# GpSimd scales and sums the gathered rows of a token tile; VectorE adds one finished sum

## The chip, the cores and the metric

The kernel runs on one core of a Trainium2 chip. The metric is device time in microseconds: the median over runs of the whole program. A TensorE, a VectorE, a ScalarE, a GpSimd and a SyncE engine work side by side in the core, each in the order of its own queue, and wait for each other on semaphores.

## What is computed

Two layers over 4 sequences of 512 tokens, width 512: a state-space mixer, a mixture of experts (64 experts, 8 for each token), a cross-attention with 16 heads, and a feed-forward part with quantized weights. The change lies in the attention stage, which also carries the end of the expert part: each token's 8 expert rows are fetched from memory, weighted and added to the residual x. In the reference, cut to that:

```python
y = lax.ragged_dot(hact, jnp.swapaxes(down_proj, 1, 2), group_sizes)
w = top_val.reshape(-1)[order]
out = jnp.zeros_like(x).at[tok].add(y * w[:, None])     # 8 rows per token
...
x = x + _L0_ffn_ref(_layernorm(x, axis=-1), ...)
x = x + _L1_xattn_ref(_layernorm(x, axis=-1), ctx_1024, ...)
...
q = rmsnorm((hidden_states @ Wq).reshape(B, Sq, H, D), gq)
scores = jnp.einsum('bqhd,bkhd->bhqk', q, k) * scale
attn = jax.nn.softmax(scores, axis=-1)
out = jnp.einsum('bhqk,bkhd->bqhd', attn, v).reshape(B, Sq, H * D) @ Wo
```

## The kernel before

`attention` (from L1421) works through 64 **units**: batch b = unit // 16, head = unit % 16. Every engine has a function `unit(pp, k)` that says, in the order of the code, what it does in a unit; nothing reorders it, so the order of the code is the order of each queue. In one unit:

- **TensorE** makes the scores of 4 query tiles (into `ps_s`, two banks), the value product of the unit before (`ps_o`), the q product of the next unit (`ps_q`), the transposes of the probabilities (`turn`, L1601), a part of the output product (`output`) and the sums of squares for the next q (`q_sums`, L1582).
- **VectorE** takes the row maxima (L1885) and makes `neg` from them and `q_rs` (L1893), takes reciprocals of the softmax sums (L1901), makes the low halves of q, prob and o (`low`, L1869), adds an output part into X (L1917) and makes `q_ms` (L1875).
- **ScalarE** takes the exponential (L1713) and the high halves (L1687).
- **GpSimd** makes the low halves of k and v (`k_part` L1779, `v_part` L1785), divides the probabilities (`normalize`, L1797) and takes the root `q_rs` (`q_root`, L1791). The root belongs to the next unit and is the last thing that the next maxima's `neg` needs.

Into this the tokens of the *next* batch are woven, for batches 0 to 2. They come as 32 rows (4 tiles of 128 tokens, 8 rows each), three per unit, in units 0 to 10 of a batch (`arriving(u, i)` names row number g, tile t and place kk among the 8). For each, GpSimd issues an indirect DMA (`gather`, L1805) from `y_dram` into one of RING = 4 slots of `got_row`, and VectorE scales it and accumulates it into X in one instruction (`gather_add`, L1928): one row ahead of the second pair of maxima, one between the first and the second `prob_t_low`, one between the third and the fourth. The three `gather` of a unit stand ahead of the first pair of `normalize`, after `v_part`, and behind `q_root`; each waits for the slot's last reader (semaphore `added`). When a tile is complete, its layer norm follows one step per unit, by `token_tile(u, lag)` and the table `STATS = (2, 5, 8, 10)`:

- lag 0, end of unit 2, 5, 8 or 10: `token_stats` on VectorE (L1937 and on),
- lag 1, the unit after: `token_root` on GpSimd (L1813), `token_norm` on VectorE (`nbias` L1971, `xn` L1975),
- lag 2: `turn_token` on TensorE, copies on ScalarE and VectorE into `x_t`.

In batches 1 to 3 the finished tiles of the batch before get their statistics in units 4 to 7 (`ended_stats`, L1953) and a root on GpSimd in unit 9. The q product of the next batch's first unit needs all four tiles.

GpSimd waits through `pool_waits`, an instruction of its own that stands in its queue. The accumulation of before:

```python
dve.wait_ge(arrived[g % RING], 16 * (g // RING + 1))
wait(dve, added, g)
dve.scalar_tensor_tensor(out=c.X[:, t, :], in0=got[:, g % RING, :],
                         scalar=m.weight[:, t, kk:kk + 1], in1=c.X[:, t, :],
                         op0=ALU.mult, op1=ALU.add).then_inc(added, 1)
```

## Time and profile before

| | us |
|---|---|
| median of 3 runs (3116.88 to 3126.09) | 3119.8 |
| the profiled execution | 3117.0 |
| its span, first to last instruction | 3115.6 |
| TensorE busy (80%) | 2485.5 |
| VectorE busy (65%) | 2025.2 |
| GpSimd busy (51%) | 1586.5 |
| ScalarE busy (40%) | 1250.8 |

The attention stage runs from about 1912 to 2920 us of the span. A share of busy time is a mean over stages with different limits; for the stage in question the rows further down show single stretches and single units. "Idle before" a group is time in which its engine waited just ahead of its instructions, with the instruction that ended the wait.

### The profile page before, as it was taken

What the parts mean: (1) busy time and instruction counts of PE and PEld (TensorE: products, weight loads), DVE (VectorE), ACT (ScalarE), POOL (GpSimd) and SP (SyncE); (2) the same over time, 40 slices, a digit from 0 to 9 for tenths busy, and PEclk for the clock granted to TensorE, in tenths of its full rate; (3) what the DMA queues carried; (4) which work ended last, traced back from release to release, by engine and by line L of the source; (5) the groups of instructions that cost most, each with busy time, mean ns of one, the idle gap of its engine ahead of it and who ended that gap; (6) DMA issues with size and microseconds to landing.
All of it is one profiled execution on the core that took longest, in us unless ns stands there. A gap on an engine that the chain in (4) does not pass through costs nothing. (4 is left out here: it accounts for less than half of the span.)

```text
span 3115.6 us, 42764 instructions
## 1 busy us (share of the span) xinstructions
PE 2485.5 (80%) x11156; PEld 1737.0 (56%) x11174; DVE 2025.2 (65%) x3184; ACT 1250.8 (40%) x2245; POOL 1586.5 (51%) x1294
## 2 busy tenths in 40 slices
PE   7825655555979489999999983889989999999686
PEld 2301212214767367667777762677777777877443
DVE  3579999897868334554444446675776676565596
ACT  3424343443345232221121212545545545555365
POOL 2446565564047666666666626654664655444110
PEclk9869899898989799999999996999999999999899
DMA  2016666653369798887777745443443543342101
GB/s 84 9 41 214 219 210 223 219 202 118 141 238 339 264 316 287 306 277 247 247 235 255 248 148 180 145 139 126 146 140 105 166 139 115 95 136 82 54 0 54
DMA packets 260696, 538.30 MB, mean 173 GB/s; under 512 B 24401, under 2 KB 90065, under 8 KB 259809
## 3 DMA queue, kind: packets, MB, share of 16 engines
q1 hardware_dynamic: 207296, 347.98, 32.9%
q0 software_dynamic: 44032, 167.80, 16.3%
q10 hardware_dynamic: 9248, 21.11, 2.0%
q8 instruction: 54, 0.88, 0.1%
q14 instruction: 66, 0.53, 0.1%
HBM read 328.14 MB, written 208.67 MB: 172 GB/s over the span
## 5 line engine op out<-in xcount | busy, mean ns | idle before, releaser
L523 PE MATMUL ps_y<-c_state,ident 128*128 128x512 f32 x512 | 268.7, 651 | 205.5 <-DVE c_state L475 205.4
L448 POOL TENSOR_TENSOR b_u<-du,bc 128x1024 f32<-128x1024 f32 x128 | 301.3, 2354 | 214.5 <-DVE c_state L475 178.0
L1713 ACT ACTIVATE prob<-ps_s,neg,q_rs 128x512 f32<-128x512 f32 x256 | 197.1, 774 | 330.5 <-DVE neg L1893 330.5
L1230 PE MATMUL ps_o<-w_dn,hid_t 96*128 x632 | 308.4, 611 | 0.0
L1797 POOL TENSOR_SCALAR prob<-prob,rden 128x512 f32<-128x512 f32 x256 | 175.6, 696 | 253.9 <-DVE rden L1901 253.9
L523 PEld LDWEIGHTS ps_y<-c_state,ident 128*128 128x128 f32 x512 | 91.8, 198 | 381.8 <-DVE c_state L475 312.7
L467 DVE TENSOR_TENSOR_SCAN state<-ps_decay,b_u 128x1024 f32<-128x1024 f32 x128 | 293.1, 2290 | 16.1 <-issue 8.7
L1266 ACT ACTIVATE silu_g<-ps_gu 128x192 f32<-128x192 f32 x159 | 52.6, 331 | 546.5 <-PE ps_gu L1211 543.0
L419 ACT ACTIVATE ps_decay<-delta,a_neg 128x511 f32 x256 | 165.9, 681 | 225.5 <-DVE state L467 225.1
L1211 PE MATMUL ps_gu<-w_gu_high,rows_t_high 128*128 (+1 forms) x636 | 230.7, 363 | 11.0 <-POOL w_gu_low L1095 9.5
L1095 POOL TENSOR_TENSOR w_gu_low<-raw_gu,w_gu_high 128x1536 fp32r<-128x1536 f32 x64 | 222.4, 3475 | 12.0 <-POOL w_gu_high L1093 12.0
L1352 DVE TENSOR_TENSOR hid<-silu_g,ps_gu 128x192 f32<-128x192 f32 x159 | 56.2, 354 | 250.4 <-ACT silu_g L1266 250.4
L1211 PE MATMUL ps_gu<-w_gu_high,rows_t_low 128*128 (+1 forms) x636 | 216.0, 340 | 0.0
L1211 PE MATMUL ps_gu<-w_gu_low,rows_t_high 128*128 (+1 forms) x636 | 215.8, 339 | 0.0
L913 POOL DMA_INDIRECT rows_dram<-xn,pos_row x128 | 126.8, 991 | 149.8 <-issue 149.8
L1687 ACT ACTIVATE prob_t_high<-ps_p 128x512 fp32r<-128x512 f32 x256 | 143.4, 607 | 130.3 <-PE ps_p L1601 130.0
L1346 DVE TENSOR_TENSOR rows_t_low<-ps_rx,rows_t_high 128x512 fp32r<-128x512 f32 x160 | 110.7, 692 | 128.1 <-ACT rows_t_high L1260 128.1
L1869 DVE TENSOR_TENSOR prob_t_low<-ps_p,prob_t_high 128x512 fp32r<-128x512 f32 x256 | 169.6, 682 | 32.7 <-ACT prob_t_high L1687 32.2
L1558 PE MATMUL ps_q<-x_t,w_q 128*128 128x512 f32 x768 | 189.6, 396 | 1.5 <-DVE x_t L1869 1.5
L475 DVE TENSOR_TENSOR c_state<-state,bc 128x1024 f32<-128x1024 f32 x128 | 189.9, 1485 | 0.0
L1558 PEld LDWEIGHTS ps_q<-x_t,w_q 128*128 128x128 f32 x768 | 147.2, 192 | 33.7 <-issue 1.9
L1885 DVE TENSOR_REDUCE high<-ps_s 128x1 f32<-128x512 f32 x256 | 163.5, 678 | 1.1 <-PE ps_s L1558 0.9
(317 smaller groups left out, 6071.5 us busy)
## 6 DMA issues: line engine op xcount, KB each, us to landing
rows_dram<-zeros SPq DMA_DIRECT2D x15, 3584.0 KB, 14.3
raw_gu<-in_gate_up POOLq DMA_DIRECT2D x64, 768.0 KB, 5.4
rows<-rows_dram SPq DMA_DIRECT2D x160, 256.0 KB, 3.9
y_dram<-y SPq DMA_DIRECT2D x158, 256.0 KB, 3.5
bc<-bc_dram SPq DMA_DIRECT2D x64, 512.0 KB, 5.8
w_q<-wq_dram SPq DMA_DIRECT2D x64, 512.0 KB, 3.7
w_o<-wo_dram SPq DMA_DIRECT2D x16, 2048.0 KB, 8.5
w_dn<-in_down POOLq DMA_DIRECT2D x64, 384.0 KB, 5.9
```

What stands on the lines that cost most here:

```text
L419: e = act.activation(decay[ec % 2][:, g * SEQ + 1:(g + 1) * SEQ], m.delta[:, ds1(b * EC + ec), 1:].rearrange("p a l -> p (a l)"), ACT.Exp, ...
L448: pool.tensor_tensor(out=b_u[:, ec % 2, :, :], in0=m.du[:, ds1(b * EC + ec), :].broadcast_to([P, G, SEQ]), in1=bc[:, par, 0, :, :], op=ALU ...
L467: dve.tensor_tensor_scan(state[:, ec % 2, :], decay[ec % 2][:, :], b_u[:, ec % 2, :, :].rearrange("p g l -> p (g l)"), 0.0, ALU.mult, ALU. ...
L475: dve.tensor_tensor(out=c_state[:, ec % 2, :, :], in0=state[:, ec % 2, :].rearrange("p (g l) -> p g l", g=G), in1=bc[:, par, 1, :, :], op= ...
L523: mm = pe.matmul(ps_y[ec][:, :], c.ident[:, :], c_state[:, ec % 2, g, :], start=False, stop=False)
L1095: pool.tensor_tensor(out=flat(w_gu[1]), in0=raw_gu[slot][:, :], in1=flat(w_gu[0]), op=ALU.subtract).then_inc(gu_ready, 1)
L1211: mm = pe.matmul(ps_gu[par][:, :], rows_t[par][x][:, k, :], w_gu[w][:, ds1(slot), k, :].rearrange("p a f -> p (a f)"), start=n == 0, stop= ...
L1230: mm = pe.matmul(ps_o[par][:, :], hid_t[par][:, k, :], w_dn[:, ds1(slot), k, :].rearrange("p a f -> p (a f)"), start=k == 0, stop=k == 1)
L1558: mm = pe.matmul(out, lhs[a], rhs[b], start=i == 0, stop=i == n - 1)
L1713: act.activation(prob[:, qt, :], ps_s[qt % 2][:, :], ACT.Exp, scale=q_rs[:, k % 2, qt:qt + 1], bias=neg[:, qt:qt + 1], accum_out=den[:, qt ...
L1797: pool.tensor_scalar(out=prob[:, qt, :], in0=prob[:, qt, :], scalar1=rden[:, qt:qt + 1], scalar2=1.0, op0=ALU.mult, op1=ALU.mult).then_inc ...
L1869: dve.tensor_tensor(out=out, in0=ps, in1=hi, op=ALU.subtract).then_inc(sem, 1)
```

## The change

VectorE's accumulations (96) go. GpSimd takes each row in two instructions: a `tensor_scalar` that multiplies the row by its weight, and a `tensor_tensor` that adds it to a sum `got_sum`, of which there are two, used in turn by tile. The first row of a tile is written scaled into the sum, with no add. VectorE adds the finished sum to X once per tile, at the head of `token_stats` (12 times), and then waits for that add. GpSimd's row steps stand behind `v_part` (the last row of the unit before), behind `q_root`, and behind the third gather. The ring of row slots has 2 in place of 4 and the steps of the tiles' layer norm come a unit later: `STATS = (3, 6, 9, 11)`. Each add waits for its own row's scaling and for the add before it; a tile's first row waits until the sum of two tiles back was taken.

```diff
-        RING, PER = 4, TOPK * ST
-        got = p.sb("got_row", [P, RING, DM])
+        RING, PER = 2, TOPK * ST
+        got, acc = p.sb("got_row", [P, RING, DM]), p.sb("got_sum", [P, 2, DM])
+        row_scaled, acc_taken = p.sem("row_scaled"), p.sem("acc_taken")
...
-        STATS = (2, 5, 8, 10)
+        STATS = (3, 6, 9, 11)
...
+            def gather_add(u, i):
+                piece = arriving(u, i)
+                if piece:
+                    g, t, kk = piece
+                    waits(arrived[g % RING], 16 * (g // RING + 1))
+                    w = m.weight[:, t, kk:kk + 1]
+                    if kk == 0:
+                        if g >= 2 * TOPK:
+                            waits(acc_taken, g // TOPK - 1)
+                        pool.tensor_scalar(out=acc[:, g // TOPK % 2, :], in0=got[:, g % RING, :], scalar1=w, scalar2=1.0,
+                                           op0=ALU.mult, op1=ALU.mult).then_inc(added, 1)
+                    else:
+                        n = g - g // TOPK
+                        pool.tensor_scalar(out=got[:, g % RING, :], in0=got[:, g % RING, :], scalar1=w, scalar2=1.0,
+                                           op0=ALU.mult, op1=ALU.mult).then_inc(row_scaled, 1)
+                        waits(row_scaled, n)
+                        waits(added, g)
+                        pool.tensor_tensor(out=acc[:, g // TOPK % 2, :], in0=acc[:, g // TOPK % 2, :], in1=got[:, g % RING, :], op=ALU.add)\
+                            .then_inc(added, 1)
...
+                if pp * U + k:
+                    gather_add(pp * U + k - 1, 2)
                 gather(pp, k, 1)
                 token_root(pp, k)
                 normalize(pp, k, 2)
                 normalize(pp, k, 3)
                 if more:
                     q_root(*nxt)
+                gather_add(pp * U + k, 0)
                 gather(pp, k, 2)
+                gather_add(pp * U + k, 1)
                 ended_root(pp, k)
...
                     dve.wait_ge(added, (n + 1) * TOPK)
+                    dve.tensor_tensor(out=c.X[:, t, :], in0=acc[:, n % 2, :], in1=c.X[:, t, :], op=ALU.add).then_inc(acc_taken, 1)
+                    dve.wait_ge(acc_taken, n + 1)
                     dve.bn_stats(bn6[:, :], c.X[:, t, :]).then_inc(t_stats, 1)
...
-                if pp * U + k:
-                    gather_add(pp * U + k - 1, 2)
...
-                gather_add(pp * U + k, 0)
...
-                gather_add(pp * U + k, 1)
```

GpSimd's queue in a plain unit of the attention stage, before, from one `q_root` to the next (`prob<-prob,rden` is `normalize`):

```order
L1791 TENSOR_TENSOR q_rs<-q_ms,power 128x4
L1805 DMA got_row<-y_dram,pos_row 128x512
L1779 TENSOR_TENSOR k_t_low<-raw_k,k_t_high 128x512
L1805 DMA got_row<-y_dram,pos_row 128x512
L1797 TENSOR_SCALAR prob<-prob,rden 128x512 x2
L1785 TENSOR_TENSOR v_s_low<-raw_v,v_s_high 128x512
L1805 DMA got_row<-y_dram,pos_row 128x512
L1797 TENSOR_SCALAR prob<-prob,rden 128x512 x2
L1791 TENSOR_TENSOR q_rs<-q_ms,power 128x4
```

The same of the changed kernel, from `q_root` on (`got_row<-got_row,weight` scales a row, `got_sum<-got_sum,got_row` adds it; its lines stand some numbers later):

```order
L1792 TENSOR_TENSOR q_rs<-q_ms,power 128x4
L1823 TENSOR_SCALAR got_row<-got_row,weight 128x512
L1827 TENSOR_TENSOR got_sum<-got_sum,got_row 128x512
L1806 DMA got_row<-y_dram,pos_row 128x512
L1823 TENSOR_SCALAR got_row<-got_row,weight 128x512
L1827 TENSOR_TENSOR got_sum<-got_sum,got_row 128x512
L1780 TENSOR_TENSOR k_t_low<-raw_k,k_t_high 128x512
L1806 DMA got_row<-y_dram,pos_row 128x512
L1798 TENSOR_SCALAR prob<-prob,rden 128x512 x2
L1786 TENSOR_TENSOR v_s_low<-raw_v,v_s_high 128x512
L1823 TENSOR_SCALAR got_row<-got_row,weight 128x512
L1827 TENSOR_TENSOR got_sum<-got_sum,got_row 128x512
```

Six instructions came in; two pairs stand between `q_root` and `k_part` and one behind `v_part`. Behind the last row shown come, as before, the third gather, the second pair of `normalize` and the next `q_root`.

VectorE's queue at the end of the unit in which the first tile's statistics are made, before (unit 2), from the first `prob_t_low` on:

```order
L1869 TENSOR_TENSOR prob_t_low<-ps_p,prob_t_high 128x4x128
L1928 SCALAR_TENSOR_TENSOR X<-got_row,weight,X 128x512
L1869 TENSOR_TENSOR prob_t_low<-ps_p,prob_t_high 128x4x128
L1875 TENSOR_SCALAR q_ms<-ps_b 128x4
L1869 TENSOR_TENSOR prob_t_low<-ps_p,prob_t_high 128x4x128
L1928 SCALAR_TENSOR_TENSOR X<-got_row,weight,X 128x512
L1869 TENSOR_TENSOR prob_t_low<-ps_p,prob_t_high 128x4x128
L1937 BN_STATS a_bn<-X 128x6
L1939 BN_AGGR a_bn<-a_bn 128x2
L1942 TENSOR_SCALAR a_vare<-a_bn 128x1
L1885 TENSOR_REDUCE high<-ps_s 128x1 x2
```

The same place in the changed kernel (unit 3):

```order
L1894 TENSOR_TENSOR prob_t_low<-ps_p,prob_t_high 128x4x128 x2
L1900 TENSOR_SCALAR q_ms<-ps_b 128x4
L1894 TENSOR_TENSOR prob_t_low<-ps_p,prob_t_high 128x4x128 x2
L1952 TENSOR_TENSOR X<-got_sum,X 128x512
L1954 BN_STATS a_bn<-X 128x6
L1956 BN_AGGR a_bn<-a_bn 128x2
L1959 TENSOR_SCALAR a_vare<-a_bn 128x1
L1910 TENSOR_REDUCE high<-ps_s 128x1 x2
```

The accumulations between the low halves are gone; the sum is added ahead of the statistics, between the last low half and the next unit's maxima.

## Rows read from the trace of the kernel before

**Rows 1.** Table of stretches: periods 1-10 of batches 0-2, a gather-free one, periods 11-13.

```profile
core 0: us, PE busy (x) PEld busy (x) DVE busy (x) ACT busy (x) POOL busy (x), PEclk, DMA share, GB/s
1938.70:2100.00 161.30, 142.87 (x702) 113.93 (x703) 112.06 (x206) 81.07 (x174) 100.33 (x104) 0.96 0.45 142
2186.10:2350.70 164.60, 147.08 (x737) 116.33 (x736) 117.26 (x218) 81.41 (x175) 101.11 (x105) 0.99 0.44 139
2437.00:2601.90 164.90, 148.13 (x736) 117.64 (x735) 117.17 (x218) 81.45 (x174) 101.07 (x104) 0.98 0.44 138
2645.80:2659.80 14.00, 13.78 (x74) 11.45 (x73) 8.02 (x16) 7.93 (x17) 6.28 (x7) 1.00 0.25 75
2601.90:2645.80 43.90, 42.10 (x217) 34.07 (x216) 27.45 (x56) 23.59 (x51) 19.49 (x23) 1.00 0.39 121
```

**Rows 2.** GpSimd's groups, 2437 to 2602: count, busy us, mean ns, idle before.

```profile
L1805 POOL DMA_INDIRECT got_row<-y_dram,pos_row x30 | 31.9, 1062 | 5.1 <-issue 3.2 <-ACT k_t_high L1687 1.3 <-DVE X L1928 0.4
L1797 POOL TENSOR_SCALAR prob<-prob,rden 128x512 f32<-128x512 f32 x40 | 27.4, 694 | 32.1 <-DVE rden L1901 32.1
L1785 POOL TENSOR_TENSOR v_s_low<-raw_v,v_s_high 128x512 fp32r<-128x512 f32 x10 | 15.9, 1589 | 0.0
L1779 POOL TENSOR_TENSOR k_t_low<-raw_k,k_t_high 128x512 fp32r<-128x512 f32 x10 | 13.0, 1300 | 0.2
L1791 POOL TENSOR_TENSOR q_rs<-q_ms,power 128x4 f32<-128x4 f32 x11 | 11.4, 1039 | 28.9 <-DVE q_ms L1875 28.9
```

**Rows 3.** VectorE's timeline, a plain period: start us, duration us, engine, line, operation.

```profile
2452.89 0.74 DVE L1928 SCALAR_TENSOR_TENSOR X<-got_row,weight,X 128x512 f32<-128x512 f32 x1
2453.55 0.68 DVE L1869 TENSOR_TENSOR prob_t_low<-ps_p,prob_t_high 128x512 fp32r<-128x512 f32 x1
...
2455.46 0.62 DVE L1893 TENSOR_TENSOR neg<-high,q_rs 128x2 f32<-128x2 f32 x1
...
2458.87 1.20 DVE L1928 SCALAR_TENSOR_TENSOR X<-got_row,weight,X 128x512 f32<-128x512 f32 x1
2460.00 1.27 DVE L1885 TENSOR_REDUCE high<-ps_s 128x1 f32<-128x512 f32 x2
```

**Rows 4.** VectorE's groups in 2437 to 2602.

```profile
L1928 DVE SCALAR_TENSOR_TENSOR X<-got_row,weight,X 128x512 f32<-128x512 f32 x30 | 28.5, 949 | 0.0
...
L1953 DVE BATCH_NORM_STATS2 f_bn<-X 128x6 f32<-128x512 f32 x4 | 2.7, 681 | 0.0
```

**Rows 5.** GpSimd's groups over the whole run, shapes kept apart.

```profile
L1095 POOL TENSOR_TENSOR w_gu_low<-raw_gu,w_gu_high 128x1536 fp32r<-128x1536 f32 x64 | 222.4, 3475 | 12.0 <-POOL w_gu_high L1093 12.0
...
L359 POOL TENSOR_TENSOR delta<-log,pos 128x512 f32 x16 | 20.2, 1265 | 4.3 <-POOL log L356 4.3
```

**Rows 6.** GpSimd's timeline in the same plain period.

```profile
2452.41 1.05 POOL L1791 TENSOR_TENSOR q_rs<-q_ms,power 128x4 f32<-128x4 f32 x1 [2.64 <-DVE q_ms L1875]
...
2458.16 1.38 POOL L1797 TENSOR_SCALAR prob<-prob,rden 128x512 f32<-128x512 f32 x2 [0.97 <-DVE rden L1901]
...
2467.54 1.04 POOL L1791 TENSOR_TENSOR q_rs<-q_ms,power 128x4 f32<-128x4 f32 x1 [2.63 <-DVE q_ms L1875]
```

**Rows 7.** TensorE's transposes and GpSimd's root in a gather-free period.

```profile
2668.89 1.03 PE L1601 MATMUL ps_p<-ident,prob 128*128 128x128 f32 x8
...
2673.83 1.02 POOL L1791 TENSOR_TENSOR q_rs<-q_ms,power 128x4 f32<-128x4 f32 x1 [2.42 <-DVE q_ms L1875]
```

**Rows 8.** VectorE and GpSimd in a token period (unit 4, batch 2).

```profile
2484.67 2.06 DVE L1971 SCALAR_TENSOR_TENSOR nbias<-a_bn,rstd 128x1 f32<-128x1 f32 x1
2486.77 0.56 DVE L1975 TENSOR_SCALAR a_xn_row<-X,rstd,nbias 128x512 f32<-128x512 f32 x1
...
2492.11 1.87 DVE L1928 SCALAR_TENSOR_TENSOR X<-got_row,weight,X 128x512 f32<-128x512 f32 x1
...
2485.40 1.30 POOL L1779 TENSOR_TENSOR k_t_low<-raw_k,k_t_high 128x512 fp32r<-128x512 f32 x1
...
2492.14 1.29 POOL L1785 TENSOR_TENSOR v_s_low<-raw_v,v_s_high 128x512 fp32r<-128x512 f32 x1
```

More of the change, by code:

```diff
@@ L1920, in before @@
                 return (pp, k - 1) if k else (pp - 1, U - 1)
-            def gather_add(u, i):
-                piece = arriving(u, i)
-                if piece:
-                    g, t, kk = piece
-                    dve.wait_ge(arrived[g % RING], 16 * (g // RING + 1))
-                    wait(dve, added, g)
-                    dve.scalar_tensor_tensor(out=c.X[:, t, :], in0=got[:, g % RING, :],
-                                             scalar=m.weight[:, t, kk:kk + 1], in1=c.X[:, t, :],
-                                             op0=ALU.mult, op1=ALU.add).then_inc(added, 1)
             def token_stats(pp, k):
```

## The prediction

> **What bounds the kernel now.** I first cut the attention stage into periods, each from one q_root (L1791) on GpSimd to the next, and read the table of stretches [rows 1]. Periods are numbered by unit within a batch; 1 to 10 of batches 0, 1 and 2 carry the gathers for the next batch. Ten of them take 161.3, 164.6 and 164.9 us; a period with no gathers takes 14.0 us, and there TensorE is busy for 13.78 of 14.00 us. So TensorE's floor is 14.0, and the gather periods stand 2.1 to 2.5 us each above it. Periods 11 to 13, which have no gathers but the last token steps, take 43.9 us together, 1.8 above three times the floor.
>
> Next, GpSimd's groups in the ten periods of batch 2 [rows 2]. It is busy 101.1 us. It idles 32.1 us for VectorE's reciprocals and 28.9 us for q_ms, and 5.1 us around the gathers. (The 11th q_ms wait, 2.6 us, belongs to the period before.) The reader should see a reserve: of 16.5 us per period GpSimd waits about 6 for VectorE. The change fills exactly this reserve, so the question is whether it fits.
>
> Then VectorE's rows of a plain period [rows 3]. Three accumulations (L1928) stand in it. The one at 2452.89 takes 0.66 us from its start to the next instruction's, the one between the first two prob_t_low the same, and the one ahead of the second pair of maxima 1.13 (2458.87 to 2460.00). Together 2.4 us of a 15.1 us period (2452.41 to 2467.54, [rows 6]).
>
> **What goes.** 96 accumulations, 30 of them in ten periods: 28.5 us of VectorE, 0.95 each [rows 4]. Of 2.4 us per period the path can keep only what lies above the 14.0 us floor: 15.1 would become 14.0. That is the largest gain of the edit, before GpSimd's price.
>
> **What comes on GpSimd.** A row now takes a scale and an add. The scale has the form of L1797: 0.69 us [rows 2]. The add has no row of its own; the nearest are L359, the same tile, two f32 operands in SBUF, 1.265 us [rows 5], and L1779, 1.30 us [rows 2]. I take 1.26. Between the two stands a wait for the scale: after a cast the same kind of wait took 12.0/64 = 0.19 us, after a tensor_tensor 4.3/16 = 0.27 [rows 5]. I take 0.19, since a one-input operation comes ahead, and keep 0.27 for the range. So a row costs 0.70 + 0.19 + 1.26 = 2.15 us; the first row of each tile has the scale alone, 0.70. Ten periods hold 30 rows, 4 of them first ones: 26 x 2.15 + 4 x 0.70 = 58.7 us. The two-step form is what makes this dear: VectorE did the pair in 0.74 us where nothing stood in its way [rows 3].
>
> **The sum for ten periods.** GpSimd's work and fixed gaps now: 101.1 + 5.1 = 106.2 us [rows 2]. v_s_low gets back what the accumulation beside it cost: 1.589 against 1.30 for the same form of k_t_low, 10 x 0.29 = 2.9 us [rows 2]. Twice per period a gather now waits for an add that has only just ended (ring of 2 instead of 4), 0.27 instead of about 0.17: 2.0 us. 106.2 - 2.9 + 2.0 + 58.7 = 164.0 us, with the dear gap and the 1.30 add 167.1. This is GpSimd with no wait for anyone, against 164.9 with 61 us of waits. Batch 1 is the same (164.6). In batch 0 GpSimd's busy time is 0.8 us less (100.3, [rows 1]): 163.2 against 161.3. The three together: -0.9, -0.6, +1.9, or +0.4 us. The whole gain on VectorE is eaten, because GpSimd becomes the bound at 16.6 us in a plain period with three pairs, where 15.1 stood; periods with a first row (1, 3, 6, 9) have 14.5 to 15.2, and the long token periods, which make the mean 16.5, get shorter.
>
> **Can GpSimd run without waits?** I followed a plain period from T, the end of q_root. GpSimd's order: row step, gather, row step, k_part, gather, normalize 0 and 1, v_part, row step, gather, normalize 2 and 3, q_root. normalize 0 is due at T + 2.15 + 0.27 + 1.06 + 2.15 + 1.30 + 0.16 + 1.0 = T+8.1. VectorE can start the maxima at about T+1.1, neg at T+2.4; if a GpSimd operation holds it up, T+4.2. From the end of neg to normalize took 2458.16 - 2456.08 = 2.1 us [rows 3, 6], so T+6.3: 1.8 us in hand. q_root is due 6.2 us after normalize 1 (1.30 + 2.15 + 0.27 + 1.06 + 1.38). Where TensorE sets the pace it takes 2673.83 - 2668.89 = 4.9 us from the start of the transposes to q_root, which q_ms releases [rows 7]: 1.2 us in hand. Plain periods stay with GpSimd.
>
> The token steps have less. L1971 (nbias) took 2.06 us: it ended at 2486.73, with GpSimd's k_t_low at 2486.70, and xn followed [rows 8]. After the change, in times from T: nbias waits for the first row's add (till T+2.2), xn for the second row's scale behind the gather (till T+4.1, and 0.5 for itself), the maxima take 1.28 (till T+5.9), neg waits for k_t_low (till T+6.9), and normalize 0 starts 2.1 later at T+9.1 where it was due at T+8.1: 1.0 us late, and GpSimd's whole order with it. That is periods 5 and 8. In batches 1 and 2 the statistics of ended tiles (L1953, 0.68 us and a small one behind it) stand there too and add 0.8 [rows 4]. So 2 x 1.0 + 4 x 1.8 = 9.2 us. **The later tiles** (STATS 3, 6, 9, 11 in place of 2, 5, 8, 10): period 11 has two row steps and the norm of unit 10 ahead of it, by the same steps as above 16.3 us. Period 12 has the sum into X and the statistics ahead of its maxima (0.74 + 0.68 and two small ones), period 13 nbias behind k_t_low (1.30) and xn (0.56) [rows 4, 8]: 1.7 to 1.9 us each, of which TensorE's cover takes some 0.4, so 15.4 each. 47.1 against 43.9 [rows 1]: 3.2 us per batch, 10 in all. Bounds of this term are 3 us (nearly all in cover) and 15.
>
> **VectorE's new add** of the finished sum, 12 times, 0.74 us or more if it waits for GpSimd's add, counts in the statistics periods (4, 7, 10, 12); I find 0.3 us in hand there and take nothing. The two added waits in GpSimd's order (sum taken, two tiles back) are long met.
>
> **Total**: 0.4 + 9.2 + 10 = +19.6 us on the profiled execution's 3117.0, so 3136.6. That execution lies 2.8 us under the median, against which the result is held; with the same difference it is 3139. I forecast **3138 us**. Some 0.3% (9.4 us) is what a measurement of this kernel can tell from none.
>
> **A rule weighed.** VectorE's accumulation took 1.87 us beside v_s_low and 0.74 beside q_root (2452.89, q_root's own row stands at 2452.41) [rows 3, 6, 8]: it stood still while GpSimd streamed SBUF. The Trainium skill (SBUF — State Buffer, Who interferes with whom) says that a VectorE instruction with two SBUF inputs and a GpSimd instruction that reads SBUF exclude each other, for a whole instruction. By this rule, which the rows bear out, removing 30 such instructions and adding 56 GpSimd ones per ten periods trades one wait for another: neg, nbias and xn remain on the path. The skill's GPSIMD Engine Reference (Elementwise) gives about 2.6 cycles per element for two inputs: an estimate of 1.1 us for 512, against 1.265 in the row; by it the sum would be some 4 us less per batch. The row decides.
>
> **Rivals.**
> A. GpSimd takes over as the bound, with late token periods: +8 to +35 us. Forecast. For it: the sum of 164 against 164.9 holds no gain, and every mis-step adds. Chance 0.55.
> B. The same bound, but token periods stay in cover and the tail costs 3 us: 0.4 + 3, with the sum's error of -3 to +3 per batch: -6 to +9 us. Chance 0.27.
> C. Faster: GpSimd's row step is much cheaper than its nearest rows (scale and add overlapping, no gap), so that it fits in the 6.1 us of waits with the chain running beside it. It decides at about 1.7 us per row (26 x 0.45 = 12 us less per batch); the floor of 14.0 caps it near -50, I price it at -15 to -50. Against it: one-input and two-input rows never stand closer than 0.18 here. Chance 0.06.
> D. Mutual blocking on every period: each of the two negs waits for a whole operation (up to 1.3), GpSimd idles for it, and a sparser TensorE loses clock (in batch 0 the granted clock was 0.96 against 1.00 in the dense stretch, [rows 1]). One more microsecond in 30 to 33 periods on top of A: +35 to +60. Chance 0.12.
>
> That the change does not do what it says I leave out: the order of both queues shows the row steps on GpSimd and none on VectorE.
>
> **How the numbers follow.** Range 3118 to 3165: below it lie C and a third of B, above it most of D, under 2 in 10. Faster 0.06 (C), same 0.27 (B), slower 0.67 (A, D).
>
> **What would show it.** Right: GpSimd's waits for the reciprocals and q_ms in periods 1 to 10 fall from 61 to under 10 us; L1823 at 0.69, L1827 at 1.26 to 1.30 with 0.19 ahead; plain periods of 16.5 us; VectorE idle longer for something it did not wait for; period 13 at 15.4. Wrong: waits for q_ms that remain above 1 us in plain periods (D), or ten periods under 160 us (C). All outside the attention stage should stay to the microsecond.

## The result and the profile after

| | before | after |
|---|---|---|
| median, us | 3119.63 (3116.88 to 3126.09, 4 runs) | 3157.23 (3150.69 to 3164.21, 4 runs) |
| span of the profiled execution | 3115.6 | 3149.2 |
| GpSimd busy | 1586.5 | 1748.7 |
| VectorE busy | 2025.2 | 1992.6 |

The changed kernel is slower: ratio 1.0118, 95% interval 1.0091 to 1.0145, or 37.6 us by the medians. The direction was forecast, and the time lies in the range. The loss was forecast at 18 us and is twice that.

All of it lies in the attention stage, as the 64 roots on GpSimd (`q_root`, one per unit) show. Both rows are the instructions of one line over the whole run: engine, operation, count, least/median/most ns, first and last start in us. First the kernel before:

```profile
L1791 POOL TENSOR_TENSOR q_rs<-q_ms,power x64: 1013/1021/1052, 1926.2 to 2887.5; 128x4 f32<-128x4 f32 x64
```

The changed kernel:

```profile
L1792 POOL TENSOR_TENSOR q_rs<-q_ms,power x64: 1011/1018/1050, 1922.9 to 2921.0; 128x4 f32<-128x4 f32 x64
```

From first to last root it was 961.3 us and is 998.1: +36.8. The spans of the profiled executions differ by 33.6 only, since the stage began 3.3 us earlier; the forecast had everything outside it unmoved to the microsecond. Below, "the stage" is this distance. A period with no gathers at the end of a batch takes 14.0 us in every kernel that follows, but each stage time is that of one profiled execution, and some periods in it depend on the granted clock: period 12 of the changed kernel took 18.0 us at 0.91 in batch 0 and 16.3 and 16.4 at 1.00 in the other two, behind the same idle of 2.07 us on TensorE. Differences of a few us in the stage are no surer than that.

The table of stretches of the changed kernel answers to [rows 1]: periods 1 to 10 of batches 0, 1 and 2, then periods 11 to 13 and a gather-free one, both of batch 2. Columns: bounds in us, length, busy us of each engine (instructions), granted TensorE clock, DMA share, GB/s.

```profile
core 0: us, PE busy (x) PEld busy (x) DVE busy (x) ACT busy (x) POOL busy (x), PEclk, DMA share, GB/s
1935.90:2104.90 169.00, 148.43 (x692) 118.66 (x692) 97.78 (x175) 80.73 (x172) 150.67 (x160) 0.91 0.45 137
2196.20:2367.70 171.50, 150.76 (x730) 118.46 (x728) 100.73 (x187) 80.85 (x172) 152.45 (x161) 0.97 0.44 133
2458.60:2630.40 171.80, 151.01 (x729) 118.49 (x727) 100.59 (x187) 80.90 (x172) 152.33 (x160) 0.97 0.43 133
2630.40:2679.40 49.00, 45.01 (x227) 36.51 (x227) 31.76 (x59) 24.56 (x53) 23.32 (x28) 0.97 0.34 108
2679.40:2693.30 13.90, 13.68 (x74) 11.39 (x73) 8.06 (x16) 7.94 (x17) 6.24 (x7) 1.00 0.25 76
```

In the ten periods of batch 2 VectorE's busy time fell from 117.2 to 100.6 us and GpSimd's rose from 101.1 to 152.3. The ten periods went from 161.3, 164.6 and 165.0 us to 169.0, 171.4 and 171.8 (+21.4, by the roots' starts), the three periods behind them from 131.6 to 147.4 over the three batches (+15.8). Outside these no period moved by more than 0.3 us but period 0 of batch 0 (12.5 to 13.0).

GpSimd's groups in the ten periods of batch 2 answer to [rows 2]: count, busy us, mean ns, idle us just before them and what ended it.

```profile
L1827 POOL TENSOR_TENSOR got_sum<-got_sum,got_row 128x512 f32<-128x512 f32 x26 | 34.5, 1326 | 7.3 <-POOL got_row L1823 7.3
L1806 POOL DMA_INDIRECT got_row<-y_dram,pos_row x30 | 32.1, 1069 | 7.5 <-POOL got_sum L1827 5.2 <-issue 1.3 <-POOL got_sum L1819 0.8
L1798 POOL TENSOR_SCALAR prob<-prob,rden 128x512 f32<-128x512 f32 x40 | 27.3, 694 | 0.6
L1823 POOL TENSOR_SCALAR got_row<-got_row,weight 128x512 f32<-128x512 f32 x26 | 18.0, 690 | 0.5
...
L1786 POOL TENSOR_TENSOR v_s_low<-raw_v,v_s_high 128x512 fp32r<-128x512 f32 x10 | 12.8, 1276 | 0.0
L1792 POOL TENSOR_TENSOR q_rs<-q_ms,power 128x4 f32<-128x4 f32 x10 | 10.4, 1040 | 5.8 <-DVE q_ms L1900 5.7
```

The waits of 61 us are gone. None is left for the reciprocals, and of the 5.7 us for `q_ms` the first (2.4) ended at the window's edge and belongs to the period before; 3.4 us are left inside, in four of ten periods. What GpSimd waits for now is mostly itself: 7.3 us between a row's scale and its add (26 times 0.28), and 7.5 around the gathers. The smaller ring makes it wait for no landing: ahead of the 26 scales it idles 0.5 us in all. A plain period shows it (GpSimd's timeline; in brackets idle time before, and what ended it):

```profile
2474.53 1.04 POOL L1792 TENSOR_TENSOR q_rs<-q_ms,power 128x4 f32<-128x4 f32 x1 [0.48 <-DVE q_ms L1900]
2475.59 0.68 POOL L1823 TENSOR_SCALAR got_row<-got_row,weight 128x512 f32<-128x512 f32 x1
2476.55 1.28 POOL L1827 TENSOR_TENSOR got_sum<-got_sum,got_row 128x512 f32<-128x512 f32 x1 [0.28 <-POOL got_row L1823]
2478.12 1.09 POOL L1806 DMA_INDIRECT got_row<-y_dram,pos_row  x1 [0.28 <-POOL got_sum L1827]
...
2490.21 1.36 POOL L1798 TENSOR_SCALAR prob<-prob,rden 128x512 f32<-128x512 f32 x2
2491.54 1.04 POOL L1792 TENSOR_TENSOR q_rs<-q_ms,power 128x4 f32<-128x4 f32 x1
```

From root to root 17.01 us with no wait for another engine. The root at 2491.54 starts the moment `normalize` ends, where before it stood 2.63 us idle for `q_ms` [rows 6]. That is the bound of the forecast, with 0.4 us more on it.

### The profile page after: what moved, and what is told of

It is laid out like the page before. It is cut to its first block and busy times, and to the rows that moved or that the text cites. A ratio compares the mean times of both kernels' runs of the same rounds, so it can differ in the third digit from the quotient of the medians.

```text
span 3149.2 us, 43057 instructions
## 1 busy us (share of the span) xinstructions
PE 2513.6 (80%) x11173; PEld 1756.1 (56%) x11174; DVE 1992.6 (63%) x3100; ACT 1251.8 (40%) x2245; POOL 1748.7 (56%) x1474
## 3 DMA queue, kind: packets, MB, share of 16 engines
q0 software_dynamic: 44032, 167.80, 16.4%
## 5 line engine op out<-in xcount | busy, mean ns | idle before, releaser
L1602 PE MATMUL ps_p<-ident,prob 128*128 128x128 f32 x1024 | 153.3, 289 | 42.2 <-POOL prob L1798 41.0
## 6 DMA issues: line engine op xcount, KB each, us to landing
rows_dram<-zeros SPq DMA_DIRECT2D x15, 3584.0 KB, 14.3
bc<-bc_dram SPq DMA_DIRECT2D x64, 512.0 KB, 5.8
w_q<-wq_dram SPq DMA_DIRECT2D x64, 512.0 KB, 4.0
```

## The experiments

Each run's stage time is its last root's start less its first. The timed ratios are against the kernel before in the same set of runs, with a 95% interval. The runs came in three sets, each on one chip with the kernel before beside it: the first four rows behind the changed kernel (before: 3122.82), the next four (3120.68), the last four. On the last chip the kernel before took 3236.26, some 115 us longer, and the first root came at 2033 to 2053 us in place of 1911 to 1936; there only ratios and the stage are compared. The intervals of e10 and of e7 overlap that of the changed kernel, so what these two are worth rests on the stage of one execution each.

| kernel | median us | ratio | stage | against before |
|---|---|---|---|---|
| before | 3119.63 | 1 | 961.3 | |
| the changed one | 3157.23 | 1.0118 | 998.1 | +36.8 |
| e2 no row work | 3108.29 | 0.993 [0.990, 0.996] | 950.8 | -10.5 |
| e3 a second scale per row | 3230.6 | 1.0329 [1.0295, 1.0363] | 1071.0 | +109.7 |
| e5 before, tiles a unit later | 3124.67 | 1.0004 [0.998, 1.0025] | 963.6 | +2.3 |
| e7 an operand in PSUM | 3147.19 | 1.0068 [1.0038, 1.0098] | 992.4 | +31.1 |
| e6 no row work, no sum | 3075.49 | 0.9854 [0.982, 0.989] | 919.9 | -41.4 |
| e10 sum added in a wait | 3150.71 | 1.0083 [1.0056, 1.0111] | 992.1 | +30.8 |
| e4 gaps filled | 3163.87 | 1.0154 [1.0086, 1.0221] | 1014.4 | +53.1 |
| e8 before, accumulations in waits | 3076.75 | 0.9852 [0.982, 0.988] | 921.9 | -39.4 |
| e13 gaps filled, operand in PSUM | 3274.5 | 1.0115 [1.0085, 1.0145] | 998.1 | +36.8 |
| e1 scale only | 3230.36 | 0.9976 [0.9952, 0.9999] | 953.5 | -7.8 |
| e12 e8 and token steps in waits | 3174.63 | 0.9807 [0.978, 0.983] | 896.7 | -64.6 |
| e14 e12, operand in PSUM | 3173.6 | 0.9803 [0.9775, 0.983] | 896.5 | -64.8 |

### What the row work costs: e2, e1, e3

Three kernels change only GpSimd's work per row. e2 leaves it out (the expert rows are then missing from X; VectorE still adds the two sums, which are set to zero once). Its edit, cut:

```diff
-                    waits(arrived[g % RING], 16 * (g // RING + 1))
-                    w = m.weight[:, t, kk:kk + 1]
...
-                        pool.tensor_tensor(out=acc[:, g // TOPK % 2, :], in0=acc[:, g // TOPK % 2, :], in1=got[:, g % RING, :], op=ALU.add)\
-                            .then_inc(added, 1)
+                    pool.wait_ge(arrived[g % RING], 16 * (g // RING + 1)).then_inc(added, 1)
```

> The changed kernel without the row steps: GpSimd issues the gathers and waits for them, but neither scales nor adds a row (the sum stays zero, so the expert rows are left out of X); VectorE still adds the sum once per tile. Theory G (GpSimd's own work sets the gather periods of the changed kernel; VectorE's and TensorE's chain would be shorter): ten gather periods of a batch fall from 171.8 to 145 to 152 us, the kernel to about 3075 to 3095 us, well under the kernel before (3119.6). Theory L (the attention chain itself did not get shorter, since the token steps and waits for the exponential stand there anyway): no lower than 3110 us.

e1 keeps the scale and leaves out the add (a sum then holds its first row alone):

```diff
-                        n = g - g // TOPK
                         pool.tensor_scalar(out=got[:, g % RING, :], in0=got[:, g % RING, :], scalar1=w, scalar2=1.0,
-                                           op0=ALU.mult, op1=ALU.mult).then_inc(row_scaled, 1)
-                        waits(row_scaled, n)
-                        waits(added, g)
-                        pool.tensor_tensor(out=acc[:, g // TOPK % 2, :], in0=acc[:, g // TOPK % 2, :], in1=got[:, g % RING, :], op=ALU.add)\
-                            .then_inc(added, 1)
+                                           op0=ALU.mult, op1=ALU.mult).then_inc(added, 1)
```

> The changed kernel with the scale of each row but without its add on GpSimd (the sum then holds only a tile's first row). GpSimd's work in a plain period is then 17.0 - 3 x (0.28 + 1.28) = 12.3 us, under the floor of 14.0. If GpSimd's own work sets the changed kernel's periods, plain periods fall to 14.0 to 14.3 and the stage to 950.8 (no row work at all) plus at most 8 us. If being held up by GpSimd's operations costs by itself, the stage stays above 965.

e3 puts one more scale, by 1.0, and the wait for it ahead of every row:

```diff
+                    pool.tensor_scalar(out=got[:, g % RING, :], in0=got[:, g % RING, :], scalar1=one[:, 0:1], scalar2=1.0,
+                                       op0=ALU.mult, op1=ALU.mult).then_inc(row_copied, 1)
+                    waits(row_copied, g + 1)
```

> The changed kernel with one more scale by 1.0 on GpSimd ahead of each row's scale, with the wait between them: 0.69 + 0.28 us more per row, 96 rows. Theory G: GpSimd has no slack in periods 1 to 10 and every bit of it shows, 0.97 x 90 = 87 us, up to 95 with period 11: 3240 to 3255 us against 3157. Theory L (GpSimd mostly waits behind VectorE instructions that its own work holds up, so more work fills idle time): at most half of it, under 3205 us.

One line of roots each (e2, e1 and e3 in this order; columns as above):

```profile
L1792 POOL TENSOR_TENSOR q_rs<-q_ms,power x64: 1013/1017/1053, 1929.2 to 2879.9; 128x4 f32<-128x4 f32 x64
```

```profile
L1792 POOL TENSOR_TENSOR q_rs<-q_ms,power x64: 1012/1017/1054, 2032.6 to 2986.1; 128x4 f32<-128x4 f32 x64
```

```profile
L1793 POOL TENSOR_TENSOR q_rs<-q_ms,power x64: 1011/1018/1049, 1933.5 to 3004.5; 128x4 f32<-128x4 f32 x64
```

The stage reads 950.8 with nothing, 953.5 with the scale, 998.1 with scale and add, 1071.0 with another scale on top. The 96 scales (66 us of GpSimd work) add 2.7 to the sum, but not because they fit in waits. Periods 1 to 3 took 0.9 to 1.5 us longer in e1 than in e2 in every batch (15.3 to 15.6 for 14.0 in batches 1 and 2, where I had expected 14.0 to 14.3), with GpSimd still waiting for VectorE. In period 2 of batch 2 (2552.41 to 2567.75) `neg` took 1.84 us, over a row's scale and the `k_t_low` that followed it at once. On the other side the twelve adds of the sum took 12.9 us in place of 20.7, and periods 4 and 7 are up to 4.1 us shorter for it. The ten periods of the three batches took 467.5 us against 468.3, and period 12, at a granted clock of 0.91 in all three batches of e1 and in one of e2, 54.0 against 50.9.

The 84 adds cost 44.6. The 96 extra scales with the waits for them, 87.6 us by GpSimd's groups, cost 72.9, and 25 us in each batch's ten periods. (The time, 3230.6, lies between the two theories, close under the first.) By e3 GpSimd is the bound of the changed kernel: more than 0.8 of what is put on it shows.

e3 also shows what the 0.28 us between scale and add are. GpSimd's timeline of e3, a later row of a tile and then a first row:

```profile
2016.40 0.68 POOL L1817 TENSOR_SCALAR got_row<-got_row,one 128x512 f32<-128x512 f32 x1
2017.28 0.70 POOL L1827 TENSOR_SCALAR got_row<-got_row,weight 128x512 f32<-128x512 f32 x1 [0.20 <-POOL got_row L1817]
2018.26 1.27 POOL L1831 TENSOR_TENSOR got_sum<-got_sum,got_row 128x512 f32<-128x512 f32 x1 [0.28 <-POOL got_row L1827]
...
2387.56 0.68 POOL L1817 TENSOR_SCALAR got_row<-got_row,one 128x512 f32<-128x512 f32 x1
2388.53 0.69 POOL L1823 TENSOR_SCALAR got_sum<-got_row,weight 128x512 f32<-128x512 f32 x1 [0.30 <-POOL got_row L1817]
```

The second scale stands behind one wait (`row_copied`) and starts 0.20 us after the first, 82 times of 84. The first row of a tile has the same scale and, from the third tile on, a second wait (`acc_taken`): 0.30 in these ten cases, 0.20 in the two without it. The add stands behind two waits, `row_scaled` and `added`: 0.28. The second wait is the one difference between the ten and the two, and what it waits for is done by then. So a second wait in the queue costs some 0.1 us even so; by an estimate from these rows 0.08 of the add's 0.28 is its second one. An add behind one wait was not run, and the 0.27 of [rows 5] stands behind a single one, in a loop of another stage, so the number of waits is not all that sets the gap.

e2 holds a surprise. With no row work at all I expected 3075 to 3095 us; it took 3108, the stage only 10.5 under before. Something on VectorE's side ate the gain of 96 removed accumulations.

### The add of the finished sum: e6, e10

e6 is e2 without VectorE's add into X and its wait:

```diff
                     dve.wait_ge(added, (n + 1) * TOPK)
-                    dve.tensor_tensor(out=c.X[:, t, :], in0=acc[:, n % 2, :], in1=c.X[:, t, :], op=ALU.add).then_inc(acc_taken, 1)
-                    dve.wait_ge(acc_taken, n + 1)
```

> As the kernel without row steps, and VectorE's add of the finished sum left out too (12 instructions and their wait; the expert rows are left out of X). In that kernel the sum's add took 2.2 us behind GpSimd's k_t_low, TensorE then stood idle for 2.5 us and the next q product ran at half the granted clock (4.50 us for 2.89), so periods 4, 7 and 12 took 18 to 20 us. If that add in its place is the cause (theory S), those periods fall to 15 to 16 us and the attention stage from 950.8 to 920 to 935 us. If the late statistics alone do it, it falls by the 12 x 0.7 us of the instruction, to about 942.

The stage fell by 30.9 us for twelve instructions of some 0.7 us, 2.6 each. Where that goes stands in e2's period 4 of batch 2. Its table of stretches, periods 3 and 4 (the second holds the add; columns as above):

```profile
2459.47:2473.50 14.03, 13.81 (x75) 11.48 (x73) 8.38 (x16) 7.82 (x17) 9.40 (x10) 1.00 0.46 134
2473.50:2492.03 18.53, 15.79 (x75) 12.50 (x73) 11.37 (x20) 7.94 (x17) 10.29 (x11) 0.91 0.66 225
```

And the timeline of e2 there, VectorE, GpSimd and TensorE (start, duration):

```profile
2475.49 2.22 DVE L1940 TENSOR_TENSOR X<-got_sum,X 128x512 f32<-128x512 f32 x1
2475.84 1.31 POOL L1780 TENSOR_TENSOR k_t_low<-raw_k,k_t_high 128x512 fp32r<-128x512 f32 x1
...
2477.75 0.69 DVE L1942 BATCH_NORM_STATS2 a_bn<-X 128x6 f32<-128x512 f32 x1
...
2478.76 1.28 DVE L1897 TENSOR_REDUCE high<-ps_s 128x1 f32<-128x512 f32 x2
...
2481.19 0.50 PE L1559 MATMUL ps_s<-k_t_high,q_t_high 128*128 128x512 f32 x1 [2.52 <-ACT prob L1714]
...
2482.75 4.50 PE L1559 MATMUL ps_q<-x_t,w_q 128*128 128x512 f32 x12
```

The same product in the kernel before, TensorE's timeline:

```profile
2491.24 2.92 PE L1558 MATMUL ps_q<-x_t,w_q 128*128 128x512 f32 x12
```

The add reads two operands in SBUF and stretches to 2.22 us over GpSimd's `k_t_low`. Statistics and then the maxima start behind it, the exponential behind those, and TensorE idles 2.52 us for it. Then the next twelve products take 4.50 us in place of 2.92, with the granted clock of the period at 0.91 against 1.00: part of it ran at 1.2 in place of 2.4 GHz. Over the twelve products alone the granted clock was 0.62. One instruction of 2.2 us on VectorE became 3.9 us of period (18.53 against 14.65 for the same period in e6). In e2 the twelve adds took 20.7 us together, 1.72 each, against 0.68 where nothing held them.

e10 asks what this is worth in the changed kernel itself. The add moves from the head of the statistics to VectorE's wait for the second pair of exponentials in the same unit:

```diff
                 maxima(pp, k, 1)
+                token_sum(pp, k)
                 reciprocals(pp, k, 1)
```

> The changed kernel with VectorE's add of the finished sum moved into its wait for the second pair of exponentials, everything else the same. Theory S and G together: in periods 4, 7 and 10 GpSimd stays the bound, so they lose only the 0.5 us by which the add held GpSimd up, and 1 us of q_ms waits; period 12 falls from 16.4 to 18.0 to about 15.5. The stage goes from 998.1 to 985 to 991 us. If the add's place doesn't matter: 998 within 2.

The groups of VectorE's add over the stage, first the changed kernel, where the twelve take 1096 ns in the mean, then e10's row by its line, 680:

```profile
L1952 DVE TENSOR_TENSOR X<-got_sum,X 128x512 f32<-128x512 f32 x12 | 13.2, 1096 | 0.0
```

```profile
L1952 DVE TENSOR_TENSOR X<-got_sum,X x12: 677/680/686, 1984.0 to 2641.7; 128x512 f32<-128x512 f32 x12
```

The stage fell by 6.0 us (992.1; I had expected 985 to 991), 5.6 of it in periods 11 to 13: period 12 took 18.0, 16.3 and 16.4 us in the three batches, with the add at 1.78 us over GpSimd's `k_t_low` in each, and takes 14.6 in each; period 11 of batch 1 rose from 17.2 to 18.5. The ten periods did not move (512.2 to 512.0 in the three batches): there GpSimd is full, and the reading is that VectorE's delay lies in its cover. So the place of this add costs about 6 us in the changed kernel; in e2, where GpSimd is not the bound, the add with its place costs 31.

The two engines hold up each other there. VectorE's and GpSimd's timeline of the changed kernel at the start of period 4, batch 2:

```profile
2508.99 0.68 DVE L1952 TENSOR_TENSOR X<-got_sum,X 128x512 f32<-128x512 f32 x1
...
2509.03 1.80 POOL L1827 TENSOR_TENSOR got_sum<-got_sum,got_row 128x512 f32<-128x512 f32 x1 [0.28 <-POOL got_row L1823]
```

VectorE's add came first and took its 0.68 us; GpSimd's took 1.80 in place of 1.28.

### The tiles a unit later: e5

e5 is the kernel before with one line changed:

```diff
-        STATS = (2, 5, 8, 10)
+        STATS = (3, 6, 9, 11)
```

> The kernel before with STATS = (3, 6, 9, 11) alone, everything else as before. If the later token steps are what the longer periods 11 to 13 cost (44 before, 49 after, per batch), this is slower than before by 10 to 16 us: 3130 to 3136. If they cost nothing by themselves and periods 11 to 13 are longer because of the row steps and the blocked steps around them, it is within 4 us of before.

No difference that can be measured (1.0004); in the stage +2.3. The three late periods take 134.8 us against 131.6 in the three batches (+3.2), and the ten before them 3.2 less; period 0 of batch 0 took 15.1 in place of 12.5. So the move of the layer norm steps is free by itself. With e6 (136.9) and e2 (143.9) the +15.8 of the changed kernel's periods 11 to 13 divides so, in this order of kernels: 3.2 the later steps; 2.1 the change from e5 to e6, which differ in the ring and in the accumulations; 7.0 the sum's add; 3.5 the row work.

### VectorE held up by GpSimd: e7

VectorE's `neg` reads 128x2 numbers from `high` and `q_rs`, both in SBUF. e7 is the changed kernel with `high` in PSUM:

```diff
-        high, neg, den, rden = (p.sb(x, [P, ST]) for x in ("high", "neg", "a_den", "rden"))
+        neg, den, rden = (p.sb(x, [P, ST]) for x in ("neg", "a_den", "rden"))
...
-        ps_q, ps_b = p.ps("ps_q", [P, SEQ]), p.ps("ps_b", [P, ST])
+        ps_q, ps_bh = p.ps("ps_q", [P, SEQ]), p.ps("ps_b", [P, 2 * ST])
+        ps_b, high = ps_bh[:, 0:ST], ps_bh[:, ST:2 * ST]
```

> The changed kernel with the row maxima kept in PSUM (beside the sums of squares), so that VectorE's product neg has one operand in SBUF and one in PSUM. If a VectorE instruction is held up by GpSimd only when both its operands are in SBUF, neg falls from a mean of 0.68 us to 0.16 in the gather periods. Theory G: the kernel gains only the 5.7 us per batch that GpSimd waits for q_ms and some of periods 11 to 13, 10 to 20 us in all: 3137 to 3147. Theory L (blocked neg is what makes it slow): 30 us or more, under 3127.

VectorE's `neg` in the ten periods of batch 2, the changed kernel and then e7:

```profile
L1918 DVE TENSOR_TENSOR neg<-high,q_rs 128x2 f32<-128x2 f32 x20 | 13.5, 676 | 0.7
```

```profile
L1919 DVE TENSOR_TENSOR neg<-ps_b,q_rs 128x2 f32<-128x2 f32 x21 | 3.3, 159 | 0.7
```

With an operand in PSUM it is never held up: 159 ns in place of 676, and 0.16 us in all 128 cases of the stage. Yet of 10 us saved per batch on VectorE the stage shows 5.7 in all, under the 10 to 20 that I had expected. The ten periods gave 6.4 us; period 12 took 18 us in all three batches, at a granted clock of 0.90 or 0.91, and gave 3.2 back. Mutual blocking exists, in nearly every period as rival D had it, but VectorE had room for most of it; it was not the larger part of what the changed kernel lost its time to.

### Filling GpSimd's gaps: e4, e13

If GpSimd is full, its own 0.28 us gaps are pure loss. e4 splits a row step and puts other work between scale and add, and between an add and the gather into its slot:

```diff
                     k_part(*nxt)
-                gather(pp, k, 0)
+                if pp * U + k:
+                    gather(*before(pp, k), 2)
+                    row_add(pp * U + k - 1, 1)
                 normalize(pp, k, 0)
                 normalize(pp, k, 1)
+                gather(pp, k, 0)
+                if pp * U + k:
+                    row_scale(pp * U + k - 1, 2)
...
-                    gather_add(pp * U + k - 1, 2)
+                    row_add(pp * U + k - 1, 2)
                 gather(pp, k, 1)
...
                     q_root(*nxt)
-                gather_add(pp * U + k, 0)
-                gather(pp, k, 2)
-                gather_add(pp * U + k, 1)
+                row_scale(pp * U + k, 0)
+                row_scale(pp * U + k, 1)
+                row_add(pp * U + k, 0)
```

> The changed kernel with GpSimd's steps in another order: each scale is kept apart from its own add by other work (the next row's scale, or v_part), and two of the three gathers from the add that they wait for. The work is the same. Theory G: the stage loses the 84 gaps of 0.28 us and about 40 of the 0.28 ahead of gathers less the usual 0.15, some 28 us if GpSimd is the bound throughout, 15 to 25 where the chain catches up: 998.1 to 973 to 983 us. If GpSimd is not the bound: within 5 us.

Plain periods fell as the gaps had it (in batch 2 period 2: 17.01 to 16.01; period 3: 15.47 to 14.70), but periods 4, 5 and 8, which have token steps, took between 18.3 and 21.2 us where the changed kernel takes between 17.5 and 18.4, and the stage by 16.3 over the changed kernel. VectorE and GpSimd in period 5 of batch 2 tell why (e4's timeline):

```profile
2549.83 3.22 DVE L1932 TENSOR_TENSOR neg<-high,q_rs 128x2 f32<-128x2 f32 x1
...
2549.82 0.71 POOL L1815 TENSOR_SCALAR got_row<-got_row,weight 128x512 f32<-128x512 f32 x1
2550.49 1.30 POOL L1786 TENSOR_TENSOR v_s_low<-raw_v,v_s_high 128x512 fp32r<-128x512 f32 x1
2551.74 1.28 POOL L1833 TENSOR_TENSOR got_sum<-got_sum,got_row 128x512 f32<-128x512 f32 x1
```

`neg`, 0.16 us by itself, took 3.22: it began with the scale and ended at 2553.05, behind three GpSimd instructions that followed each other without a gap. It did not come in between the first and the second. Such cases are in the changed kernel too (its timeline, VectorE and GpSimd, period 1 of batch 2; `prob` x2 are two instructions):

```profile
2466.56 2.57 DVE L1918 TENSOR_TENSOR neg<-high,q_rs 128x2 f32<-128x2 f32 x1
...
2466.49 1.37 POOL L1798 TENSOR_SCALAR prob<-prob,rden 128x512 f32<-128x512 f32 x2
2467.82 1.27 POOL L1786 TENSOR_TENSOR v_s_low<-raw_v,v_s_high 128x512 fp32r<-128x512 f32 x1
2469.08 0.69 POOL L1823 TENSOR_SCALAR got_row<-got_row,weight 128x512 f32<-128x512 f32 x1
```

Here it came in between `v_s_low` and the scale, which has no gap ahead of it. The Trainium skill (SBUF — State Buffer, Who interferes with whom) says that a VectorE instruction with two SBUF inputs contends with a GpSimd instruction that reads SBUF, and that issue order decides who blocks; the trace agrees with the first, and with the second where GpSimd's add took 1.80 us behind VectorE's. The trace also shows that a waiting VectorE instruction can be passed over by GpSimd's next one. Over the changed kernel's stage no held `neg` was passed over at a gap of 0.28 us, and eight ended in the one between scale and add; where no gap stood it was passed over 13 times and came in about as often, so a gap is not needed, and which of the two happens stays open. That the gaps made the changed order the better one fits these counts and was not tested apart from them.

e13 is e4 with `high` in PSUM, the edit of e7:

> The kernel with GpSimd's gaps filled (stage 1014.4 us against 998.1 of the changed kernel), with the row maxima in PSUM, so that neg has one operand in SBUF. In the filled order neg took 1.72 and 3.22 us in a token period, the latter through three GpSimd operations that stood back to back (scale, v_s_low, add). If that is what made the filled order slower (theory P: a VectorE instruction with two SBUF operands gets no turn while GpSimd's operations follow each other without a gap), the token periods fall from 19 to 21 to under 18 us and the stage to 970 to 985. If the filled order is slow for another reason (gathers that land late, the moved third row), it stays above 1005.

Its roots:

```profile
L1793 POOL TENSOR_TENSOR q_rs<-q_ms,power x64: 1012/1017/1052, 2047.7 to 3045.7; 128x4 f32<-128x4 f32 x64
```

The stage is 998.1, 16.3 under e4, and no better than the changed kernel; I had expected 970 to 985. The same operand in PSUM had given 5.7 us in the unfilled order, so of the 16.3 that the filled order lost some 10.6 went through `neg`, and 5.7 (e13 against e7) did not. Other instructions with SBUF operands are still held up in the token periods: `nbias`, 0.15 us by itself, took up to 4.11 in e13 (period 7 of batch 1, 21.8 us) and at most 1.27 in e7. That they make up the rest is argued, not shown.

### The waits that were VectorE's own: e8, e12, e14

VectorE sits idle ahead of its reciprocals while ScalarE makes the exponentials. In the kernel before this was 34.0 us in the ten periods of batch 2, 1.70 us for each pair (VectorE's groups, 2437 to 2602):

```profile
L1901 DVE RECIPROCAL rden<-a_den 128x2 f32<-128x2 f32 x20 | 3.3, 166 | 34.0 <-ACT prob L1713 34.0
```

e8 is the kernel before, with its three accumulations per unit moved there and nothing given to GpSimd:

```diff
-        STATS = (2, 5, 8, 10)
+        STATS = (3, 5, 8, 11)
...
                 maxima(pp, k, 0)
+                if pp * U + k:
+                    gather_add(pp * U + k - 1, 1)
                 reciprocals(pp, k, 0)
...
+                maxima(pp, k, 1)
                 if pp * U + k:
                     gather_add(pp * U + k - 1, 2)
-                maxima(pp, k, 1)
+                gather_add(pp * U + k, 0)
                 reciprocals(pp, k, 1)
...
-                gather_add(pp * U + k, 0)
                 turned(pp, k, 1)
...
-                gather_add(pp * U + k, 1)
                 turned(pp, k, 3)
```

> The kernel before with VectorE's accumulations moved into its two waits for the exponentials (1.70 us each per unit): one row behind the first neg, two behind the second; STATS = (3, 5, 8, 11) since a row is added later. If the accumulations cost 2.4 us of the path per plain period and the waits hold them, plain periods fall from 15.1 to 15.5 to the floor of 14.0 and the stage from 961.3 to 915 to 935 us. If GpSimd's operations hold them up there too (two SBUF operands), they lengthen the waits and the stage stays above 945.

VectorE's timeline in a plain period of e8, and this kernel's row in the table of stretches for a period with three accumulations:

```profile
2426.39 0.74 DVE L1928 SCALAR_TENSOR_TENSOR X<-got_row,weight,X 128x512 f32<-128x512 f32 x1
2428.16 0.17 DVE L1901 RECIPROCAL rden<-a_den 128x2 f32<-128x2 f32 x1 [1.03 <-ACT prob L1713]
...
2431.12 1.60 DVE L1928 SCALAR_TENSOR_TENSOR X<-got_row,weight,X 128x512 f32<-128x512 f32 x2
```

```profile
2408.82:2422.82 14.00, 13.78 (x75) 11.48 (x73) 10.43 (x19) 7.82 (x17) 10.26 (x10) 1.00 0.42 135
```

The first accumulation takes 0.74 us out of a wait of which 1.03 are still left; plain periods stand at 14.0 us with TensorE busy 13.78, the same as a period with no gathers at all [rows 1]. The stage is 39.4 us shorter than before, within 2 us of e6 (41.4), which has no accumulations. They had cost little but their place. (The STATS line is not what did it: e5, with a like shift alone, gained nothing.)

e12 moves the tokens' statistics and norm there too, with their root on GpSimd in the same unit:

```diff
-        STATS = (3, 5, 8, 11)
+        STATS = (3, 6, 9, 11)
...
                     gather_add(pp * U + k - 1, 1)
+                token_stats(pp, k)
+                token_norm(pp, k)
                 reciprocals(pp, k, 0)
...
                 turned(pp, k, 3)
-                token_stats(pp, k)
-                token_norm(pp, k)
...
             def token_root(pp, k):
-                tok = token_tile(pp * U + k, 1)
+                tok = token_tile(pp * U + k, 0)
```

> The kernel with the accumulations in VectorE's waits (stage 921.9 us), with the token statistics and the token norm moved there too, behind the first neg, the root half a unit earlier and STATS = (3, 6, 9, 11). Periods with a token step stand at 14.5 to 18.2 us; if 1 to 1.9 us of VectorE ahead of the maxima is what lengthens them, those without ended-tile statistics fall to 14.0 to 14.8 and the stage to 900 to 912. If the copies and transposes of the tokens or blocked instructions hold them, less than 6 us comes off.

> The same with the row maxima in PSUM. neg has 0.2 to 0.5 us of waiting for GpSimd in some 60 of 128 cases; where the period is TensorE's nothing comes of it, elsewhere up to 0.4 us per period: 0 to 8 us off the stage.

The roots of e12:

```profile
L1791 POOL TENSOR_TENSOR q_rs<-q_ms,power x64: 1013/1019/1050, 2053.0 to 2949.6; 128x4 f32<-128x4 f32 x64
```

The stage of e12 is 896.7 us, 64.6 under before, ratio 0.9807 [0.978, 0.983]: with e14 the best kernel of the study. I had expected 900 to 912. Its ten periods take 139.3, 144.2 and 144.2 us; ten times 14.0 is the floor of the forecast. e14 is e12 with the PSUM operand of e7 and gains nothing more (896.5): here, where VectorE has slack, its being held up costs nothing that shows.

## Why the direction was right and the size was not

**What bounds the kernel now**: right, but read too briefly. Waits of GpSimd (61 us in ten periods) were read as the reserve to fill. VectorE's own waits, 34.0 us for the exponentials in the same ten periods, were not looked at; e8 shows that the accumulations fit into them without GpSimd. That changes nothing in the forecast of this change, but it is what the change should have been measured against.

**What goes**: right. Of the 2.4 us in a plain period only what stands above the floor can come off, and e8 and e6 show periods at 14.0.

**What comes on GpSimd**: this is the step that failed, by the size of its terms. A row step was priced at 2.15 us and took 2.30. The scale is 0.69 us, counted at 0.70. Ahead of the add stand 0.28 us, where I took 0.19 and kept 0.27 for the range: 26 x 0.09 = 2.3 us in batch 2. I had chosen between two rows by the kind of operation that comes ahead; e3 shows that behind the same one-input scale it is 0.20 with one wait and 0.28 to 0.30 with two, and the code has two ahead of the add. The waits were not counted. The add, taken at 1.26, is 1.28 alone and 1.326 in the mean, since two of 26 ran beside VectorE's add of the sum and took some 0.5 longer: 26 x 0.066 = 1.7 us. Gathers wait 7.5 where 7.1 was counted. Together 4.4: GpSimd without waits takes 171.8 - 3.4 = 168.4 us, forecast 164.0. `v_s_low` came back to 1.276, forecast 1.30.

**Can GpSimd run without waits**: right in the main. Waits inside the ten periods are 3.4 us, forecast 3.6, though not quite where I put them: 1.1 in period 5, 0.5 in period 8, and 1.3 in period 7 and 0.5 in period 1, which I had not named. The ten periods of batches 0, 1 and 2 came out 3.8, 3.8 and 4.2 us over my working, 11.8 in all: of +21.4 I had 9.6. (Of the 61 us of waits that were to be filled, 2.6 lay outside the ten periods; the sum does not use them.)

**The later tiles**: mis-sized. 16.3, 15.4 and 15.4 were forecast for periods 11, 12 and 13. In the three batches period 11 took 50.1 (48.9 forecast), period 12 50.7 (46.2) and period 13 46.6 (46.2): 15.8 us over before in place of 10. Most of the difference is period 12, and in it the add of the sum: priced at 0.74 us, it took 1.78 over `k_t_low`, TensorE then idled 2.07 us, and in batch 0 the granted clock of the period was 0.91. That a lone add with two SBUF operands would be held up, as `nbias` was, stood in [rows 8] and was not applied to it. With the add elsewhere (e10) the period takes 14.6, under the 15.4 forecast.

**VectorE's new add** "take nothing": no loss shows in periods 4, 7 and 10, where e10 left the ten periods of the three batches at 512.0 for 512.2; in period 12 it does, as said. e10's 6.0 us and the 5.8 that periods 11 to 13 were short are near each other by chance: moving the add also takes away the 0.74 that the forecast had in it, and period 11 grew.

**The ledger**: forecast +19.6, measured +36.8 in the stage. Of the missing 17.2 are 11.8 in the ten periods (row step and gathers) and 5.8 in periods 11 to 13 (mostly the sum's add in period 12); the rest of the stage took back 0.4. Three batches multiply each small mis-size: 0.09 us on a gap, 78 times, is 7 us.

**The rivals**: A's mechanism was the case, but not its price: +36.8 lies just above its +8 to +35 and inside D's +35 to +60, so that the time fell within the whole range owes something to D's share of it. B needed token periods in cover and did not come. C needed 1.7 us per row; it was 2.30. D's blocking was there, and e7 priced that of `neg` at 5.7 us in the stage; its sign, waits for `q_ms` above 1 us in plain periods, did not come (0.5 at most). The granted clock of the ten periods fell, as it had it, from 0.96, 0.99 and 0.98 to 0.91, 0.97 and 0.97; with GpSimd as the bound there no run tells what that cost.

## What to carry to other kernels

Before work moves to another engine, look for the waits of the engine that has it now. Here the same accumulations cost some 40 us where they stood, about 2 a few instructions further on, and more than they had cost once they were on GpSimd. Once a queue is full nearly all that is added to it shows, and before that its work can still lengthen the chain by holding up another engine: count every gap between dependent instructions, with the number of waits in it, and multiply by all repetitions. A lone instruction ahead of a critical one is priced by what it is held up by, and by the idle that it gives TensorE, not by its own duration.

## What the runs showed of the hardware

- A 128x512 scale on GpSimd that waits for the scale just before it starts 0.20 us after that one's end with one wait in the queue, 0.30 with two (e3); an add behind a scale and two waits 0.28, in all 84 cases of the changed kernel.
- A VectorE instruction with two SBUF operands can be held up through several GpSimd instructions that stand back to back: `neg`, 0.16 us with an operand in PSUM, took 3.22 us through three. None was passed over at a gap of 0.28 us; where there was no gap both happened.
- It works both ways: GpSimd's add took 1.80 us in place of 1.28 where VectorE's add ran first.
- An idle of 2.52 us on TensorE was followed by twelve products at 4.50 in place of 2.92 us, at a granted clock of 0.62 over them. Behind an idle of 2.07 us in period 12 of the changed kernel the clock fell in one batch and held in two: 18.0 us against 16.3 and 16.4.
